# Gathered expert rows and late row tiles turned by VectorE and transfers in place of TensorE

## The reference

```python
# cross attention: 16 heads, q from the 512 rows, k and v from ctx, all rms-normed
q = rmsnorm(h @ Wq, gq); k = rmsnorm(ctx @ Wk, gk); v = ctx @ Wv
x = x + tanh(g_xattn[1]) * (softmax(q @ k.T * scale) @ v) @ Wo

# mixture of experts: E=16, I=352, 4 experts per token
xs = h[tok]                                  # 2048 rows, sorted by expert
h_act = silu(xs @ gate_w[e].T) * (xs @ up_w[e].T)
x = x + tanh(g_ffn[1]) * zeros.at[tok].add((h_act @ down_w[e].T) * w)
```

## Time and profile before

| | |
|---|---|
| median of 3 runs | 1406.72 us (1406.38 to 1410.99) |
| the profiled execution, its own time | 1406.11 us |
| its span, first to last instruction | 1404.3 us |
| busy: TensorE matmuls | 1376.5 us, 98% of the span |
| busy: VectorE / ScalarE / GpSimd | 1140.6 / 976.5 / 942.4 us |
| 16 DMA engines, hardware queue | 42.7% of their span |
| granted TensorE clock | 0.998 |
| chain that ended last | PE 76% of the span, DVE 3%, POOL 2%, ACT 2% |

### The profile page before, as it was taken

One profiled execution on the slowest core, in us unless ns is written; L12 is line 12 of the kernel. 1 busy time (PEld: TensorE's weight loads), 2 busy tenths in 40 slices (PEclk: granted clock), 3 DMA queues, 4 the chain that ended last, 5 costly groups with the idle time before them and its releaser, 6 DMA issues.

```text
span 1404.3 us, 23125 instructions
## 1 busy us (share of the span) xinstructions
PE 1376.5 (98%) x7614; PEld 1175.1 (84%) x7614; DVE 1140.6 (81%) x2072; ACT 976.5 (70%) x2165; POOL 942.4 (67%) x729
## 2 busy tenths in 40 slices
PE   8899999999999999999999999999999999999998
PEld 6778778888888888888888888888888888877886
DVE  7888778788888888887878888887878787888777
ACT  7863467788876767667676767667676766666764
POOL 4876557777776567667676767676776757776561
PEclk9999999999999999999999999999999999999999
DMA  9420023333433555656564646566565653442312
GB/s 338 156 78 16 23 75 107 106 117 116 122 113 113 167 167 183 190 168 193 176 200 156 204 160 189 183 179 188 174 198 163 189 170 125 138 145 94 98 61 90
DMA packets 135734, 204.59 MB, mean 146 GB/s; under 512 B 10112, under 2 KB 70528, under 8 KB 135616
## 3 DMA queue, kind: packets, MB, share of 16 engines
q1 hardware_dynamic: 131856, 190.79, 42.7%
q0 software_dynamic: 3760, 12.32, 3.3%
HBM read 157.72 MB, written 45.35 MB: 145 GB/s over the span
## 4 chain that ended last, share of the span: by engine, by line
PE 76%; DVE 3%; POOL 2%; ACT 2%; DMA 1%; issue 1%; SPq 0%; ACTq 0%; POOLq 0%
PE j_bank L578 9%; PE j_bank L580 9%; PE j_bank L579 9%; PE w_bank L578 8%; PE w_bank L580 8%; PE w_bank L579 8%; PE s_bank L578 4%; PE s_bank L580 3%; PE s_bank L579 3%; PE t_bank L655 3%; PE t_bank L613 2%; PE t_bank L578 1%; PE t_bank L579 1%; PE t_bank L580 1%; PE w_bank L761 1%
## 5 line engine op out<-in xcount | busy, mean ns | idle before, releaser
L1032 ACT ACTIVATE prob<-s_bank,neg_bias,q_scale 128x512 f32<-128x512 f32 x255 | 197.4, 777 | 141.5 <-DVE neg_bias L1545 141.5
L1613 DVE SCALAR_TENSOR_TENSOR x_sb<-w_bank,inv_sum,x_sb 128x512 f32<-128x512 f32 x254 | 186.7, 745 | 32.0 <-PE w_bank L580 30.9
L1947 POOL TENSOR_TENSOR xnT_lo<-xnT_raw,xnT_hi 128x512 fp32r<-128x512 f32 (+2 forms) x47 | 126.4, 2691 | 63.1 <-ACT xnT_hi L990 63.1
L1524 DVE TENSOR_REDUCE neg_max<-s_bank 128x1 f32<-128x512 f32 x255 | 168.0, 679 | 0.9 <-PE s_bank L580 0.9
L578 PE MATMUL j_bank<-wkv_lo,cT_hi 128*128 128x256 f32 x512 | 145.0, 283 | 0.0
L1947 POOL TENSOR_TENSOR cT_round<-cT_raw,x_round 128x1408 fp32r<-128x1408 f32 (+1 forms) x31 | 104.4, 3367 | 59.9 <-ACT x_round L990 59.9
L580 PE MATMUL j_bank<-wkv_hi,cT_lo 128*128 128x256 f32 x512 | 144.4, 282 | 0.0
L579 PE MATMUL j_bank<-wkv_hi,cT_hi 128*128 128x256 f32 x512 | 144.2, 282 | 0.0
L1988 POOL TENSOR_TENSOR q_scale<-q_ss,minus_half 128x4 f32<-128x4 f32 x64 | 66.0, 1031 | 106.3 <-DVE q_ss L1537 106.3
L1947 POOL TENSOR_TENSOR sqs_lo<-xn,sqs_hi 128x512 fp32r<-128x512 f32 x62 | 104.0, 1677 | 34.5 <-ACT xn L1120 33.8
L1580 DVE STREAM_TRANSPOSE prob<-prob 128x1024 f32<-128x1024 f32 x59 | 73.5, 1245 | 60.8 <-ACT prob L1032 60.4
(11 more groups left out here) (312 smaller groups left out, 4600.2 us busy)
## 6 DMA issues: line engine op xcount, KB each, us to landing
turn<-prob SPq DMA_DIRECT2D x59, 512.0 KB, 3.1
prob<-turn SPq DMA_DIRECT2D x236, 128.0 KB, 3.2
stage<-w SPq DMA_DIRECT2D x96, 256.0 KB, 3.5
xnT_raw<-w_gu SPq DMA_DIRECT2D x31, 704.0 KB, 4.5
cT_raw<-w_gu SPq DMA_DIRECT2D x31, 704.0 KB, 5.9
xnT_raw<-w_dn SPq DMA_DIRECT2D x16, 768.0 KB, 5.4
cT_raw<-w_dn SPq DMA_DIRECT2D x15, 768.0 KB, 5.4
planes<-bits SPq DMA_DIRECT2D x16, 512.0 KB, 5.0
```

Of the source, the lines that this page charges most:

```text
L1032: nc.scalar.activation(dst, src, ACT.Exp, bias=neg_bias[:, u % 2, i:i + 1], scale=q_scale[:, u % 2, i:i + 1], accum_out=row_sum[:, u % 2, ...
L1524: nc.vector.tensor_reduce(neg_max[:, u % 2, i:i + 1], score_bank(t, i)[:], AX_X, ALU.max, negate=True).then_inc(own_max, 1)
L1613: nc.vector.scalar_tensor_tensor(out=here, in0=w_bank[0][:] if packed else out_bank(t, i)[:], scalar=inv_sum[:, w % 2, i:i + 1], in1=here, ...
L1947: return nc.gpsimd.tensor_tensor(dst, src, hi, ALU.subtract)
```

## The change

TensorE no longer turns the gathered rows of blocks 1 to 30, nor the 12 late tiles. Both go the way of the probability pair: 32x32 turns on VectorE, a store to `turn_dram`, a load in four transfers.

- **Late tiles.** `late_norm` writes its tile in block order and moves in ScalarE's step from the front to the place just ahead of the softmax. VectorE turns the tile (`late_turn`) where it made the low part. SyncE stores it (`store_late`, ahead of `store_pair`) and loads it (`load_late`, behind `load_pair`, ahead of the weights). `late_copy` of the tile before moves to the place ahead of `late_norm`, reads SBUF in place of PSUM, and the low part goes to GpSimd.
- **Rows.** VectorE turns `row_raw` (`turn_rows`) behind `values_lo` of the same step in which it is gathered. SyncE stores it ahead of `store_pair` and loads it behind `load_pair`; a loaded run is 32 elements long. `row_raw` is now the source of `rows_to_hi` and `rows_to_lo`, so the next gather waits for `rows_to_lo`; that moves ahead of `gate_up_lo` on VectorE, and `rows_to_hi` ahead of `gate_up_hi(0)` on ScalarE.
- `load_pair` waits on a semaphore that the row store counts up too. `turn_dram` has four planes in place of two.

```diff
+STORES = [MOVES[u] + min(max(u + 1 - T0, 0), NB - 1) for u in range(NI + 1)]
 # SyncE
             def load_pair(u):
-                sp.wait_ge(p_stored, 16 * (MOVES[u] + 1))
+                sp.wait_ge(p_stored, 16 * (STORES[u + 1] if in_block(u + 1) else STORES[u] + 1))
+            def store_rows(n):
+                sp.wait_ge(rows_turned, n)
+                wait(sp, rows_moved, 16 * NT * (n - 1))
+                sp.dma_start(turn_dram[3], row_raw).then_inc(p_stored, 16)
+            def load_rows(n):
+                sp.wait_ge(p_stored, 16 * STORES[T0 + n - 1])
+                for c in range(NT):
+                    sp.dma_start(row_raw[c * QUAD:(c + 1) * QUAD, :].rearrange("a (j r m) -> a j r m", j=DT, r=NT),
+                                 turn_dram[3].rearrange("(r a) (j c m) -> c a j r m", r=NT, c=NT, j=DT)[c]).then_inc(
+                                     rows_moved, 16)
                 if in_block(t):
+                    store_rows(b + 1)
                     store_pair(t - 1)
                     down_weights(b, e)
                     load_pair(t - 1)
+                    load_rows(b + 1)
...
                 if not in_block(t):
+                    store_late(t)
                     store_pair(t - 1)
                     load_pair(t - 1)
+                    load_late(t)
 # TensorE
-                    if t in LATE and i == 1:
-                        pe.wait_ge(late_lo, t - LATE_HEAD + 1)
+                        if t in LATE_NEEDED:
+                            pe.wait_ge(late_lo, LATE_NEEDED[t])
-                    late_turn()
-                turn_rows()
+                turn_first_rows()
 # ScalarE
-                late_norm()
                 if not in_block(t - 1):
                     moved_hi(w)
                 if packed:
+                    rows_to_hi()
                     gate_up_hi(0)
-                    rows_to_hi()
...
                 first_rows()
-                late_copy()
+                late_copy(t - 1)
+                late_norm()
                 softmax(0)
 # VectorE
+                def turn_rows():
+                    dve.wait_ge(rows_in, 16 * (b + 2))
+                    nc.vector.transpose(row_raw, row_raw).then_inc(rows_turned, 1)
...
                     inverses()
+                    rows_to_lo()
                     gate_up_lo()
                     squares_out()
-                    rows_to_lo()
                     copy_y()
                     shift(0)
                     shift(1)
                     values_lo()
+                    turn_rows()
                     turn_quads()
...
-                late_lower()
+                late_turn()
 # GpSimd
-                    wait(pool, rows_mm, n)
+                    if n == 1:
+                        pool.wait_ge(rows_mm, 1)
+                    else:
+                        wait(pool, rows_lo, n)
...
                 gate_up_lo()
+                late_lower(t - 1)
                 scale_keys()
```

More of the change, by code:

```diff
@@ L93 @@
 LATE_HEAD = min(LATE)
+LATE_NEEDED = {next(t for t, item in enumerate(ITEMS) if item[1] == b): NT * b for b in range(1, B)}
 XN, XNS = numbered("df", ACT_ORDER)
@@ L809, in project_down @@
                     last.then_inc(d_mm, 1)
-                def late_turn():
-                    if t not in LATE:
-                        return
-                    pe.wait_ge(late_normed, t - LATE_HEAD + 1)
-                    need(pe, w_added, 4, w, 0)
-                    for j in range(DT):
-                        last = pe.transpose(w_bank[1][:, j * P:(j + 1) * P], late_row(t)[:, j * P:(j + 1) * P], ident[:])
-                    last.then_inc(late_turned, 1)
                 def key_values():
@@ L1654, in rows_to_lo @@
                     dve.wait_ge(rows_hi, b + 1)
-                    lower(rowT[1], w_bank[1][:], f32(rowT[0])).then_inc(rows_lo, 1)
+                    lower(rowT[1], row_raw if b else w_bank[1][:], f32(rowT[0])).then_inc(rows_lo, 1)
+                def turn_rows():
+                    if not (up and b + 1 < NB):
+                        return
+                    dve.wait_ge(rows_in, 16 * (b + 2))
+                    nc.vector.transpose(row_raw, row_raw).then_inc(rows_turned, 1)
                 def inner(half):
@@ L2055, in squares_lo, with late_lower @@
                     lower(sqs[1][:], squares(t), f32(sqs[0][:])).then_inc(sq_lo, 1)
+                def late_lower(v):
+                    if v not in LATE:
+                        return
+                    pool.wait_ge(late_hi, v - LATE_HEAD + 1)
+                    lower(late_tile(1, v), late_blocks(v), f32(late_tile(0, v))).then_inc(late_lo, 1)
                 if t == 0:
@@ L2209 @@
     x0 = nc.dram_tensor("x0", (S, D), F32, kind="Internal").ap()
[L2210 removed]
+    turn = nc.dram_tensor("turn", (4, P, S), F32, kind="Internal").ap()
     flamingo_kernel(nc, *args, x0, rows, y, turn, out)
```

73 lines of the change are left out of this document (47 added, 26 removed).

## The result

| | before | after |
|---|---|---|
| median | 1408.33 us, 4 runs (1406.38 to 1410.99) | 1437.87 us, 4 runs (1436.73 to 1441.93) |
| span of the profiled execution | 1404.3 us | 1436.6 us |

The ratio is 1.0211, with a 95% interval of 1.0192 to 1.0229: the change makes the kernel 30 us slower. 1414 was forecast, with a range up to 1430. The sign was right, the size was not.

What follows compares the result with a forecast made beforehand. TensorE was taken to set the pace, with other rings close below. From 1406.7 us, +5 for late steps and +2 for block steps gave 1413.7, forecast 1414 us; own range 1407 to 1428, overall range 1398 to 1430.

Steps and rivals of the forecast that it cites:

- What bounds the kernel: Late and block steps: TensorE is busy throughout, 16.14 and 22.57 us, and sets the pace until another ring becomes as long.
- What leaves TensorE: Late and block steps: four turns cost 0.44 us; removing them saves 18.5 us in all if nothing else moves.
- Late ring: Late steps, through SyncE: four more load issues delay the output projection's weights; 16.7 us a step against 16.14, +5 us.
- Block rings 1 and 2: Block steps: VectorE's changed order and the gather's later start; at most 2.4 us faster, the gather covered.
- Ring 1: Block steps, VectorE's order: `rows_to_lo` ahead of `squares_out` delays `gate_up(1)`; 0.08 of 0.44 us saved is left.
- Ring 2: Block steps: the gather starts when `rows_to_lo` is done and lands 5.3 us later, covered by 0.1 us.
- Block ring 3: Block steps: `down_weights`, issued behind the pair's store, lands before `down_hi` needs it, with slack of 0.5 us by medians.
- The first chunk: Next block's first weight chunk: issued near 713.6 behind four more loads, still in time, covered by 0.1 to 1 us.
- I take 0.15 us a step: Block steps: allowance for slower transfers in two rings with 0.1 and 0.3 us of cover, 4.5 us in all.
- Rival C: Row loads: short runs of 128 bytes clog the transfers and make the first chunk late; 1443 us, half that 1428; chance 0.10.
- Rivals A and B: Whole kernel: A, the saving comes through, 1388 us, half of it 1397; B, a wash, 1406 us; chance 0.15 each.

Runs made afterwards that it cites:

- `late_last`: Only the late tiles changed, expert rows as before the change, with the four late loads behind the step's weight loads on SyncE's queue; 1405.57 us, ratio 0.9976.
- `no_trip`: The changed kernel without the store and the four loads of the turned rows; 1424.4 us.
- `port_order`: `port` with the row copies back in their old places, reading a buffer of fixed content, so that the gather need not wait for them; 1411.8 us.
- `port`: `no_trip` with GpSimd's lowering of `wkv` moved behind its squares in the block steps; 1420.9 us.
- `long_runs`: The changed kernel with the four row loads of a block written as runs of 128 elements instead of 32; 1430.1 us.
- `two_buf`: The changed kernel with a separate buffer for turned rows, old copy order, row and late loads issued later, GpSimd's `wkv` behind its squares; 1402.9 us, ratio 0.9956.

## Why the prediction was right or wrong

- **What bounds the kernel.** Right as far as it went: TensorE set the pace, with rings close under it. That work taken from it "is worth its time until another ring of waits becomes as long as the step" is what happened.
- **What leaves TensorE, 0.44 us for four turns.** Right for the late steps, where 15.70 was reached once nothing stood in the way. Too much for the block steps: even with no trip and no changed order, 22.33 and 22.61 were reached and not 22.13. By the weight loads' idle times, the turns there covered some 0.3 us of waiting, for GpSimd among others.
- **Late ring, 16.7 us a step, +5 us.** Right: 16.5 us in the mean and +3.7 to +5.2 in the seven kernels that have it, with the wait that the prediction named (ScalarE ahead of `wo_hi`, 27.1 us in 11 steps), and `late_last` takes it away. The single steps vary from 15.7 to 17.8, which was not foreseen, so that the mean came so close is partly luck.
- **Block rings 1 and 2, -2.4 us for the order and nothing for the gather.** This step failed, and by itself is worth 13.2 us: `no_trip`, in which only these rings and VectorE's turn are left of the change, has block steps 10.8 us longer than before where 2.4 shorter were forecast. `port_order`, with the order and the gather where they were, has them 3.2 shorter.
  - *Ring 1, `rows_to_lo` ahead, 0.08 of 0.44 us left.* The way is right: it is the one in the chain of `port`. The size fits two of three steps of `no_trip` (22.55 against 22.49), which may be chance, since no run has this ring alone. The sum had no term for VectorE standing still beside GpSimd, up to 0.76 us more (2.26 for 1.50 us in `no_trip`) in every third step, in a VectorE order with no gap to take it up.
  - *Ring 2, the gather, "covered by 0.1 us".* Mis-sized. VectorE waited for it in 7 of 19 blocks of the changed kernel and in 13 of `port`, up to 1.0 us. The landing was right (5.40 in the chain against 5.3), but GpSimd starts it 0.28 us behind the end of `rows_to_lo` (945.19 to 945.47), which is more than the cover. How the 13.2 us divide between the two rings stays open.
- **Block ring 3, the third chunk.** Right that it is covered: ScalarE waited 1.7 us for it in 4 of 19 blocks.
- **The first chunk, "covered by 0.1 us at that end, by 1 us if it lands in 4.5".** This step failed too, and the other half of the error is here (16.9 us with the trip, less the 4.5 allowed for all covers, is 12.4). It was to go out at 713.6, 8.4 us behind the end of a pair's turn at 705.2. It went out 9.1 us behind it in steps of the same kind. The difference is the row loads' issue, 2.62 us where 1.89, the price of `load_pair`, was put. That kind has one attention weight load ahead of the chunk; with two of them it is 9.6. Before the change that could not be seen in the chunk's own start, which is 6.8 to 7.0 us behind the turn in all three kinds, because the queue was idle ahead of it (710.20 to 711.65 in the step read). The row loads used that idle time up, and from there on their longer issues and a second weight load count in full. The issue is not all of it: in `long_runs`, where the four loads take the 1.87 us that the prediction allowed, the trip still costs 6.2 us.
- **"I take 0.15 us a step."** The number had no row behind it. (The bounds of the two parts would also add up to 1406 to 1430 and not to the own range of 1407 to 1428; nothing hangs on it.) Covers of 0.1, 0.3 and 0.1 to 1 us on three joined rings were treated as three small risks. They are on one path: gather, turn of the rows, turn of the pair, store, eight issues, chunk, split, and by the softmax and the third chunk back to `rows_to_lo` two steps on. In the chain shown, the lateness of one is not absorbed before the next.
- **Rival C, short runs, 1443 (0.10).** It was nearest in time (1443 against 1438) and had the place, the first chunk late by about 1 us. What it had wrong is where a short run costs: in the issue and not in the transfer, and by a factor of 1.4 and not of 2. `long_runs` puts the short runs' share at 10.7 us, a third of the loss, and the landing times of 2.9 and 3.0 us say that the transfer took no part in it.
- **Rivals A and B** did not come. `late_last` and `two_buf` point to what A needed, no queue, no order and no buffer changed on the way, but neither comes near its 1388 to 1397 us.

## What to carry to other kernels

Before an operation is moved from the engine that bounds a kernel to a longer way round, write the whole way as one ring (buffer free, gather, turn, store, loads, next user, buffer free again) and add it up with its queue time; covers of single pieces can't be weighed one by one if the pieces are in one ring. Issue time counts like work: put new transfers behind the ones that are waited for, and give them a buffer of their own, so that no order has to be changed for their sake. And a saving on the bounding engine is worth no more than the distance to the next operand it waits for.

## What the hardware showed that I had not expected

- Issuing a DMA holds SyncE longer if its runs are short: 0.66 us for 64 KB in 32-element runs against 0.47 us in 128-element runs (2.62 and 1.87 us for four), with the same bytes.
- VectorE's instruction with two SBUF operands stands still while a GpSimd instruction on SBUF runs: a 128x1024 low part takes 1.08 us plus what is left of GpSimd's, 1.39 to 2.29 us in the kernels of before and after, `no_trip` and `port`. GpSimd's gather instruction takes 1.05 us beside a VectorE reduction from PSUM and 2.18 beside a lowering from SBUF.
- With the turns gone, TensorE's weight loads waited 0.3 us for GpSimd where they had not waited before. So matmul rows that say 100% busy do not show how near the next wait is.
